# One-head attention: queries and keys through one folded matrix

## The chip, the cores and the metric

The kernel runs on one core of a Trainium2 chip. The metric is the time of one execution on the device in microseconds (us). The core has five engines with queues of their own that run in order and wait for each other by semaphores: TensorE (PE; PEld for its weight loads), VectorE (DVE), ScalarE (ACT), GpSimd (POOL) and SyncE (SP), which issues the DMAs.

## What is computed

Sixteen batches of 256 rows by 256 features pass through four conditioned blocks; the change touches the attention of the last one only. Cut to it, the reference is:

```
h = layernorm(x) * (1.0 + g1) + be1
Q = h @ Wq + bq
K = h @ Wk + bk
V = h @ Wv + bv
scores = einsum('bsd,btd->bst', Q, K) / sqrt(256)
attn = softmax(scores, axis=-1) @ V
x = x + a1 * attn
```

All weights are 256 by 256, there is one head, and everything is fp32.

## The kernel before

The work is done in eight stages, one behind the other, each over all 16 batches: feed-forward stages 0, 1, 3, 4, 5 and 7, a 16-head attention (2) and the one-head attention (6), which is meant here by "the stage". A batch is held as two tiles of 128 rows. To keep fp32 precision with the faster one-pass type (fp32r), every operand is split into a high part and the rest, its low part, and every product is three matmuls, low by high, high by low, high by high (`split3`, lines 290 to 292). So each matrix that TensorE makes is read twice from its bank: ScalarE writes the high part, VectorE the low part, and what needs the matrix waits for the low part.

The order of the work is written out by hand. The stage is a row of turns (`sh_turn`); in turn b, while batch b goes through its probabilities, batch b+1 goes through its projections and scores, and batch b+2 through its normalization. TensorE's order in a turn is: transposes of the normalized rows of b+2 (`ln_transpose`, line 418), query and key projection of b+1 (`sh_qk`), transposes of the probabilities of b (`sh_transpose`, line 1469), value projection of b+1 (`sh_v`), scores of b+1 (`sh_scores`), weighted sum of b (`sh_values`). VectorE's order is: statistics of b+3, reciprocal and scaling of b (lines 1501, 1503), residual update, low parts of queries and keys (line 1573), low part of the transposed probabilities (1483), low part of the values (1586), maximum of the scores (1489) and its scaled negative (1493), low part of the normalized rows (439), the next slice of the weights of stage 7 (328). GpSimd normalizes b+3 (367, 369, 377), makes the two residual additions (1217, 1209) and the low part of the weights (335). SyncE's queue loads the next slice of weights when GpSimd is done with the last one, and behind that the gate row of the batch (1222), for which GpSimd's line 1209 waits.

Ahead of the turns `sh_start` does the projections and the scores of batch 0. Ahead of that lies the last group of the feed-forward stage 5: at its end TensorE has two hidden chunks to multiply out (`ff_output`), and the head of the next stage is transposed in between; VectorE then updates the group's result (`ff_take`, line 648) and GpSimd adds it to x (665). `sh_v_hi` of batch 0 waits for those additions.

Of the kernel before, what the change touches and what calls it, by code (L numbers as in the profile page):

```python
# [23 lines left out]
P = 128  # L24
# [19 lines left out]
def bass_cond_blocks(nc, t, out):  # L44
# [62 lines left out]
    with ctx:  # L107
# [40 lines left out]
        gates = sb("gates", [P, 2 * GB, 2 * D], scope=ffn)  # L148
        ffn.close()
# [46 lines left out]
        be = sb("be", [P, 2, DC, BATCH])  # L196

# [42 lines left out]
        b_q = sem("b_q"); b_k = sem("b_k"); b_v = sem("b_v")  # L240
        q_hi = sem("q_hi"); q_lo = sem("q_lo"); k_hi = sem("k_hi"); k_lo = sem("k_lo")
# [23 lines left out]
        def after_attention(name, eng, p):  # L265

            values = HEADS * BATCH + (BATCH if p == L3_FF else 0)
            if name == "tensor":
                eng.wait_ge(w_lo, SLICE_BASE[p + 1])
                eng.wait_ge(exp_ready, values)  # L270
                if p == L3_FF:
                    eng.wait_ge(q_lo, BATCH)
                    eng.wait_ge(k_lo, BATCH)
# [473 lines left out]
        def ff_body(name):  # L747
            def body(eng, p, g, i, left):
# [20 lines left out]
                for c in range(C):  # L769
# [7 lines left out]
                    if name == "tensor":  # L777
# [10 lines left out]
                        ff_output(eng, p, g, i, c)  # L788
                    if name == "scalar":
# [7 lines left out]
                        if p == L3_FF and c == 1 and prev:  # L797
                            ff_gelu2(eng, p, g - 1)
                    if name == "vector":
# [28 lines left out]
                if name == "vector":  # L828
                    if ends:
                        head_unit(name, eng, p + 1, 0)  # L830
                    if last_norms:
# [3 lines left out]
                if name == "gpsimd":  # L835
                    if prev and p == L3_FF:
                        ff_gate2(eng, p, g - 1, 1 - i)
# [604 lines left out]
        qk1, kk1 = qk  # L1442
# [41 lines left out]

        def sh_max(dve, b):
# [24 lines left out]
        def sh_qk(pe, b, j, which):  # L1510
            (w, _) = w_tiles(S6)
            pe.wait_ge(ln_lo, S6 * BATCH + b + 1)
            B, lo, s = ((QB, q_lo, b_q), (KB, k_lo, b_k))[which]
            if not early(b, 1):
                pe.wait_ge(lo, b)
            for m in range(DC):
                for c in range(DC):
                    col = which * D + m * P
                    last = split3(pe, B[:, m * SEQ:(m + 1) * SEQ], [v[:, c, col:col + P] for v in w],
                                  [a[:, c, :] for a in a1[j]], c == 0, c == DC - 1)  # L1520
            last.then_inc(s, 1)
# [33 lines left out]
        QK_OF = ((QB, qk1, b_q, q_hi, q_lo, 0), (KB, kk1, b_k, k_hi, k_lo, DC))  # L1555

        def sh_qk_hi(act, b):
            for B, dst, mm, hi, _, at in QK_OF:
                act.wait_ge(mm, b + 1)
                act.wait_ge(s_mm, H0 + b)  # L1560
                for m in range(DC):
                    n = BIAS_AT[S6] + at + m
                    l = act.activation(dst[0][:, m * SEQ:(m + 1) * SEQ], B[:, m * SEQ:(m + 1) * SEQ],
                                       ACT.Identity, bias=vecs[:, n:n + 1])
                l.then_inc(hi, 1)

        def sh_qk_lo(dve, b):
            for B, dst, _, hi, lo, at in QK_OF:
                dve.wait_ge(hi, b + 1)
                for m in range(DC):  # L1570
                    n = BIAS_AT[S6] + at + m
                    cols = slice(m * SEQ, (m + 1) * SEQ)
                    l = dve.scalar_tensor_tensor(dst[1][:, cols], B[:, cols], vecs[:, n:n + 1],
                                                 dst[0][:, cols].bitcast(F32), ALU.add, ALU.subtract)
                l.then_inc(lo, 1)
# [33 lines left out]
        def sh_turn(name, eng, b, i, left):  # L1609
# [3 lines left out]
            if name == "tensor":  # L1613
                if b:
                    sh_ln(name, eng, b + 2, i)
                if left >= 1:
                    sh_qk(eng, b + 1, n, 0)
                    sh_qk(eng, b + 1, n, 1)
# [3 lines left out]
                if left >= 1:  # L1622
                    sh_v(eng, b + 1, n)
                    sh_scores(eng, b + 1)
                sh_values(eng, b, i)
            if name == "scalar":
                sh_scale1(eng, b)
                if left >= 1:
                    sh_qk_hi(eng, b + 1)
# [6 lines left out]
            if name == "vector":  # L1636
# [5 lines left out]
                if left >= 1:  # L1642
                    sh_qk_lo(eng, b + 1)
# [23 lines left out]
        def sh_start(name, eng):  # L1667
# [6 lines left out]
            for b in range(2):  # L1674
# [3 lines left out]
                if b == 0:  # L1678
                    if name == "tensor":
                        sh_qk(eng, 0, 0, 0)  # L1680
                        sh_qk(eng, 0, 0, 1)
                        sh_v(eng, 0, 0)
                    if name == "scalar":
                        sh_qk_hi(eng, 0)
                        sh_v_hi(eng, 0, 0)
                    if name == "vector":
                        sh_qk_lo(eng, 0)
                        sh_v_lo(eng, 0, 0)
            if name == "tensor":
                sh_scores(eng, 0)  # L1690
# [144 lines left out]
```

## Time and profile before

| | us |
|---|---|
| three runs, median | 1705.23 |
| lowest, highest | 1705.14, 1708.14 |
| the profiled execution | 1705.73 |
| its span, first to last instruction | 1703.9 |

| engine | busy, us | share of the span |
|---|---|---|
| TensorE, matmuls | 1618.7 | 95% |
| TensorE, weight loads | 1469.1 | 86% |
| VectorE | 1247.3 | 73% |
| ScalarE | 1181.5 | 69% |
| GpSimd | 941.0 | 55% |

The mean granted clock of TensorE is 0.982 of full speed. The shares are means over all stages; what the change is worth is read from the one stage and the end of the one ahead of it. Matmuls overlap, and their recorded ends are modelled, so that the distance from one start to the next says what a matmul costs, and its recorded length does not.

### The profile page before, as it was taken

The numbers are of one execution on the slowest core, as the hardware profiler recorded it, in microseconds if no ns is written. First come the engines' busy times: TensorE is split into PE (matmuls) and PEld (weight loads), VectorE is DVE, ScalarE is ACT, GpSimd is POOL, SyncE is SP. The second block draws the span as 40 slices with busy tenths as digits, with TensorE's granted clock in tenths as the row PEclk, the third lists the DMA queues.
The fourth block names the chain that finished last, engine by engine and source line by source line (L and its number), as shares of the span: only waits on it lengthen the run. The fifth ranks groups of instructions, "written<-read, shape, count | busy, mean of one in ns | idle before, by whom it ended". The sixth has DMA issues, their size and how long they took to land. (4 is left out here: it accounts for less than half of the span.)

```text
span 1703.9 us, 37905 instructions
## 1 busy us (share of the span) xinstructions
PE 1618.7 (95%) x13539; PEld 1469.1 (86%) x13539; DVE 1247.3 (73%) x2701; ACT 1181.5 (69%) x2944; POOL 941.0 (55%) x1139
## 2 busy tenths in 40 slices
PE   4888988999999999999999899999999999989997
PEld 2547878999999999999999789998888899979997
DVE  4766867888888888888888755556787778854442
ACT  3545657888888888888888665566667567756663
POOL 1555664666666666666666533323656578832222
PEclk7999999999999999999999899999999999999999
DMA  9223220000000000000000011111112212211111
GB/s 308 56 63 89 75 59 8 6 10 11 11 11 11 11 11 11 11 11 11 11 11 11 15 34 32 32 32 25 56 46 60 52 29 48 48 44 51 36 40 50
DMA packets 110974, 65.96 MB, mean 39 GB/s; under 512 B 81530, under 2 KB 92788, under 8 KB 110788
## 3 DMA queue, kind: packets, MB, share of 16 engines
q1 hardware_dynamic: 110788, 63.54, 13.9%
q8 instruction: 110, 1.80, 0.4%
q14 instruction: 76, 0.62, 0.1%
HBM read 59.06 MB, written 4.46 MB: 37 GB/s over the span
## 5 line engine op out<-in xcount | busy, mean ns | idle before, releaser
L1097 POOL TENSOR_TENSOR prob<-prob,rinv 128x512 f32<-128x512 f32 x254 | 259.1, 1041 | 51.1 <-DVE rinv L1078 51.1
L1069 ACT ACTIVATE prob<-s_banks,nmax 128x256 f32<-128x256 f32 x512 | 235.8, 475 | 6.7 <-DVE nmax L1059 6.7
L290 PE MATMUL bank<-WBhi,hl 128*128 128x256 f32 x768 | 219.2, 285 | 5.8 <-DVE upd L648 5.0
L291 PE MATMUL bank<-WBlo,hh 128*128 128x256 f32 x768 | 217.6, 283 | 0.0
L292 PE MATMUL bank<-WBhi,hh 128*128 128x256 f32 x768 | 215.4, 281 | 0.0
L611 ACT ACTIVATE hh<-bank,vecs 128x512 fp32r<-128x512 f32 x120 | 82.8, 690 | 154.0 <-PE bank L292 154.0
L1059 DVE TENSOR_REDUCE nmax<-s_banks 128x4 f32<-128x1024 f32 x128 | 156.4, 1222 | 45.0 <-issue 42.0
L1128 ACT ACTIVATE pthi<-bank 128x512 fp32r<-128x512 f32 x256 | 138.9, 595 | 69.0 <-PE bank L1118 68.6
L431 ACT ACTIVATE nThi<-bank,mod 128x256 fp32r<-128x256 f32 x192 | 110.4, 575 | 101.1 <-issue 75.6
L290 PE MATMUL bank<-aThi,WAlo 128*128 128x256 f32 x576 | 175.3, 304 | 2.4 <-DVE qklo L1026 2.4
L1133 DVE TENSOR_TENSOR ptlo<-bank,pthi 128x512 fp32r<-128x512 f32 x256 | 164.9, 686 | 4.4 <-ACT pthi L1128 0.5
L617 DVE TENSOR_TENSOR hl<-bank,hh 128x512 fp32r<-128x512 f32 x120 | 82.4, 688 | 112.2 <-ACT bank L611 111.2
L290 PEld LDWEIGHTS bank<-WBhi,hl 128*128 128x128 f32 x768 | 145.7, 190 | 18.5 <-issue 9.4
L291 PE MATMUL bank<-aTlo,WAhi 128*128 128x256 f32 x576 | 161.5, 280 | 0.0
L292 PE MATMUL bank<-aThi,WAhi 128*128 128x256 f32 x576 | 161.1, 280 | 0.0
L291 PEld LDWEIGHTS bank<-WBlo,hh 128*128 128x128 f32 x768 | 145.8, 190 | 6.9
L292 PEld LDWEIGHTS bank<-WBhi,hh 128*128 128x128 f32 x768 | 146.5, 191 | 0.0
L377 DVE TENSOR_SCALAR xn<-x,meanvar,rstd 128x256 f32<-128x256 f32 x224 | 120.9, 597 | 30.2 <-POOL rstd L369 30.2
L611 ACT ACTIVATE hh<-s_banks,vecs 128x512 fp32r<-128x512 f32 x120 | 84.2, 702 | 72.8 <-PE s_banks L292 72.1
L1144 PE MATMUL bank<-ptlo,vv 128*128 128x256 f32 x512 | 129.1, 285 | 4.6 <-DVE of L1170 4.6
L617 DVE TENSOR_TENSOR hl<-s_banks,hh 128x512 fp32r<-128x512 f32 x120 | 81.6, 680 | 70.6 <-ACT s_banks L611 70.6
L1177 POOL CAST oThi<-of 128x256 fp32r<-128x256 f32 x128 | 50.9, 397 | 141.2 <-DVE of L1170 140.3
(185 smaller groups left out, 5723.7 us busy)
## 6 DMA issues: line engine op xcount, KB each, us to landing
gates<-gate_scratch SPq DMA_DIRECT2D x96, 256.0 KB, 3.6
agate<-gate_scratch SPq DMA_DIRECT2D x32, 256.0 KB, 3.6
stage<-in_L_cond_W SPq DMA_DIRECT2D x64, 64.0 KB, 2.3
out<-x SPq DMA_DIRECT2D x16, 256.0 KB, 2.2
adaw<-in_L_cond_Wc SPq DMA_DIRECT2D x1, 3072.0 KB, 17.7
stage<-in_L_cond_W_qkv SPq DMA_DIRECT2D x8, 384.0 KB, 3.4
x<-in_x SPq DMA_DIRECT2D x1, 2560.0 KB, 16.6
stage<-in_L_cond_ff_w SPq DMA_DIRECT2D x32, 64.0 KB, 2.1
```

The lines of the kernel that those rows point to most:

```text
L290: pe.matmul(dst, lhs[1], rhs[0], start=start, stop=False, skip_group_check=True)
L291: pe.matmul(dst, lhs[0], rhs[1], start=False, stop=False, skip_group_check=True)
L292: return pe.matmul(dst, lhs[0], rhs[0], start=False, stop=stop, skip_group_check=True)
L377: last = eng.tensor_scalar(xn[j][:, k * D:(k + 1) * D], x[:, bass.ds(b * ROWW + k * D, D)], meanvar[:, j, k, 0:1], rstd[:, j, k:k + 1], AL ...
L611: last = act.activation(dst[:, :], U_BANKS[r][:, :], ACTF[p], bias=vecs[:, at:at + 1])
L617: dve.tensor_tensor(hl[r][:, :], U_BANKS[r][:, :], hh[r][:, :].bitcast(F32), ALU.subtract).then_inc(h_lo, 1)
L1059: dve.tensor_reduce(nmax[n % 2][:, :], s_banks[:, :, :].rearrange("p h (q k) -> p (h q) k", q=TPB), AX_X, ALU.max, negate=True).then_inc(n ...
L1069: last = act.activation(prob[h % 4][:, q, :], SB_[h % 2][:, q * SEQ:(q + 1) * SEQ], ACT.Exp, bias=of_head(nmax, h)[:, q:q + 1], accum_out= ...
L1097: pool.tensor_tensor(prob[h % 4][:, :, :], prob[h % 4][:, :, :], scale, ALU.mult).then_inc(prob_ready, 1)
L1128: act.activation(pt[h % 4][0][:, :], PTB[h % 2][:, :], ACT.Copy).then_inc(pt_hi, 1)
L1133: dve.tensor_tensor(pt[h % 4][1][:, :], PTB[h % 2][:, :], pt[h % 4][0][:, :].bitcast(F32), ALU.subtract).then_inc(pt_lo, 1)
L1144: last = pe.matmul(OB[:, h % 2 * SEQ:(h % 2 + 1) * SEQ], vv[:, c, h * P:(h + 1) * P], pt[h % 4][m][:, c * SEQ:(c + 1) * SEQ], start=c == 0 ...
```

## The change

The scores are written with one matrix: with h the modulated rows, Q K^T = (h (Wq Wk^T) + Wk bq) h^T + a term that depends on the query row alone, h Wq bk + bq bk. The changed kernel forms Wq Wk^T (`keyed`, split in high and low part, over a free piece of the weights' tile), Wk bq (`wkey`), Wq bk (`wrow`) and bq bk (`bdot`) once, at the end of stage 5: `fold_tensor`, `fold_scalar`, `fold_vector`. TensorE transposes the two weight matrices there in 16 steps, eight behind each of the output chunks 1 and 2, multiplies them in 12 matmuls behind chunk 3, and forms the vectors in 16 full-fp32 matmuls of one column and one of two.

In the stage, `sh_q` takes the place of the query projection, and the key projection, its two ScalarE and two VectorE operations and the wait of the scores for the keys are gone; the scores multiply by h itself. `sh_r` adds eight matmuls a batch, with parts of h as weights and two columns to stream, for the row term; `sh_row` takes it on VectorE in three operations. `sh_max` subtracts the row term from the scaled maximum and adds it again, in two operations where there was one.

```diff
         def sh_max(dve, b):
...
+            dve.wait_ge(r_scaled, b + 1)
+            dve.scalar_tensor_tensor(smax[0][:, :], smax[0][:, :], -SCALE1, rows_scaled[:, :], ALU.mult, ALU.subtract
+                                     ).then_inc(row_max, 1)
+            dve.wait_ge(row_max, b + 1)
             dve.wait_ge(exp_ready, n - 1)
-            dve.tensor_scalar(nmax[0][:, 0:TPB], smax[0][:, :], -SCALE1, None, ALU.mult).then_inc(nmax_ready, 1)
+            dve.tensor_tensor(nmax[0][:, 0:TPB], smax[0][:, :], rows_scaled[:, :], ALU.add).then_inc(nmax_ready, 1)
...
+        def sh_row(dve, b):
+
+            dve.wait_ge(b_r, b + 1)
+            dve.wait_ge(fold_cols, 3)
+            pairs = RB[:, 0:2 * TPB].rearrange("p (q v) -> p q v", v=2)
+            dve.tensor_copy(rowr[:, :], pairs[:, :, 0]).then_inc(r_taken, 1)
+            dve.wait_ge(r_taken, 2 * b + 1)
+            dve.scalar_tensor_tensor(rowr[:, :], pairs[:, :, 1], bdot[:, 0:1], rowr[:, :], ALU.add, ALU.add).then_inc(r_taken, 1)
+            dve.wait_ge(r_taken, 2 * b + 2)
+            dve.tensor_scalar(rows_scaled[:, :], rowr[:, :], SCALE1, None, ALU.mult).then_inc(r_scaled, 1)
...
+        def sh_r(pe, b, j):
+            if b:
+                pe.wait_ge(r_taken, 2 * b)
+            else:
+                pe.wait_ge(fold_cols, 3)
+            for q in range(TPB):
+                for c in range(DC):
+                    for a in a1[j]:
+                        last = pe.matmul(RB[:, 2 * q:2 * q + 2], a[:, c, q * P:(q + 1) * P], wrow[:, c, :],
+                                         start=c == 0 and a is a1[j][0], stop=c == DC - 1 and a is a1[j][1], skip_group_check=True)
+            last.then_inc(b_r, 1)
...
-        def sh_scores(pe, b):
+        def sh_scores(pe, b, j):
             pe.wait_ge(q_lo, b + 1)
-            pe.wait_ge(k_lo, b + 1)
...
                                   [m[:, c * SEQ + q * P:c * SEQ + (q + 1) * P] for m in qk1],
-                                  [m[:, c * SEQ:(c + 1) * SEQ] for m in kk1], c == 0, c == DC - 1)
+                                  [a[:, c, :] for a in a1[j]], c == 0, c == DC - 1)
...
+        def fold_vector(dve):
+
+            dve.tensor_tensor(bprod[:, :], vecs[:, BQ:BQ + DC], vecs[:, BK:BK + DC], ALU.mult).then_inc(fold_prod, 1)
+            dve.wait_ge(fold_hi, 1)
+            dve.tensor_tensor(keyed[1], FOLD_A[:, :].rearrange("p (k m) -> p k m", k=DC), keyed[0].bitcast(F32),
+                              ALU.subtract).then_inc(fold_lo, 1)
+            dve.wait_ge(fold_mm, 2)
...
+            for at, tiles, bias in ((0, wT[0:2], BK), (DC, wT[2:4], BQ)):
+                for m in range(DC):
+                    for d in range(DC):
+                        for v in tiles:
+                            pe.matmul(bank[6][:, at + m:at + m + 1], v[:, d * D + m * P:d * D + (m + 1) * P].bitcast(F32),
+                                      vecs[:, bias + d:bias + d + 1], start=d == 0 and v is tiles[0],
+                                      stop=d == DC - 1 and v is tiles[1], skip_group_check=True)
```

TensorE in a turn, before: the end of the key projection (`vv` holds the normalized rows of every second batch, `WAhi`, `WAlo` the weights), the transposes of the probabilities, the first matmul of the values.

```order
L290 MATMUL bank<-vv,WAlo 128x256
L291 MATMUL bank<-vv,WAhi 128x256
L292 MATMUL bank<-vv,WAhi 128x256
L1469 MATMUL bank<-ident,prob 128x128 x4
L290 MATMUL s_banks<-WAhi,vv 128x256
```

The same place now: the end of the one projection, the row term, the transposes, the values.

```order
L301 MATMUL bank<-vv,WAlo 128x256
L302 MATMUL bank<-vv,WAhi 128x256
L303 MATMUL bank<-vv,WAhi 128x256
L1629 MATMUL bank<-wrow,vv 128x2 x8
L1553 MATMUL bank<-ident,prob 128x128 x4
L301 MATMUL s_banks<-WAhi,vv 128x256
```

The twelve matmuls of the keys are gone, and eight of two columns stand between projection and transposes.

VectorE in the first turn, from the low parts of queries and keys (four operations) to the scaled maximum, before:

```order
L1573 SCALAR_TENSOR_TENSOR qklo<-bank,vecs,qkhi 128x256 x4
L1483 TENSOR_TENSOR ptlo<-bank,pthi 128x512
L1586 TENSOR_TENSOR vv<-s_banks,vv 128x512
L1489 TENSOR_REDUCE smax<-s_banks 128x2
L1493 TENSOR_SCALAR nmax<-smax 128x2
```

The same place now (`rowr`, `rows_scaled`: the row term):

```order
L1677 SCALAR_TENSOR_TENSOR qklo<-bank,wkey,qkhi 128x256 x2
L1574 COPY rowr<-bank 128x2
L1576 SCALAR_TENSOR_TENSOR rowr<-bank,bdot,rowr 128x2
L1578 TENSOR_SCALAR rows_scaled<-rowr 128x2
L1567 TENSOR_TENSOR ptlo<-bank,pthi 128x512
L1690 TENSOR_TENSOR vv<-s_banks,vv 128x512
L1584 TENSOR_REDUCE smax<-s_banks 128x2
L1588 SCALAR_TENSOR_TENSOR smax<-smax,rows_scaled 128x2
L1592 TENSOR_TENSOR nmax<-smax,rows_scaled 128x2
```

Two operations of 256 columns went, three of two columns came between the low parts, and one behind the maximum.

VectorE at the beginning of the stage, before: the last hidden chunk's low part, the low part of batch 0's normalized rows, then the update of the last feed-forward group (`upd`) and the statistics of batch 2.

```order
L617 TENSOR_TENSOR hl<-s_banks,hh 128x512
L439 TENSOR_TENSOR aTlo<-bank,aThi 128x512
L648 TENSOR_TENSOR upd<-bank,gates 128x512 x2
L354 BN_STATS stats<-x 128x6 x2
L360 BN_AGGR meanvar<-stats 128x2 x2
```

The same place now (`WAlo<-bank,WAhi` is the low part of the folded matrix):

```order
L628 TENSOR_TENSOR hl<-s_banks,hh 128x512
L450 TENSOR_TENSOR aTlo<-bank,aThi 128x512
L1515 TENSOR_TENSOR bprod<-vecs 128x2
L1517 TENSOR_TENSOR WAlo<-bank,WAhi 128x512
L1520 CAST wrow<-bank 128x2
L1521 COPY wkey<-bank 128x2
L1522 COPY bprod<-bank 128x2
L1524 TENSOR_TENSOR wrow<-bank,wrow 128x2
L1526 TENSOR_TENSOR bdot<-bprod 128x1
L659 TENSOR_TENSOR upd<-bank,gates 128x512 x2
L365 BN_STATS stats<-x 128x6 x2
```

Seven operations of the fold stand ahead of the update, and the second of them waits for ScalarE's high part of the product.

## Rows read from the trace of the kernel before

**Rows 1.** Stretches, one turn: us, busy time of each engine, clock, DMA share, GB/s
```profile
1431.47:1439.82 8.35, 8.32 (x70) 8.07 (x69) 6.82 (x19) 6.05 (x16) 6.97 (x8) 1.00 0.25 47
```

**Rows 2.** Timeline of TensorE, the same turn: start, us, line, operation
```profile
1431.47 0.60 PE L418 MATMUL bank<-ident,xn 128*128 128x128 f32 x4
...
1431.91 0.39 PE L290 MATMUL bank<-aThi,WAlo 128*128 128x256 f32 x1
...
1432.14 0.28 PE L291 MATMUL bank<-aTlo,WAhi 128*128 128x256 f32 x1
...
1434.83 0.60 PE L1469 MATMUL bank<-ident,prob 128*128 128x128 f32 x4
...
1435.19 0.36 PE L290 MATMUL s_banks<-WAhi,aTlo 128*128 128x256 f32 x1
...
1436.88 0.36 PE L290 MATMUL s_banks<-qkhi,qklo 128*128 128x256 f32 x1
...
1438.38 0.28 PE L290 MATMUL bank<-vv,ptlo 128*128 128x256 f32 x1
...
1439.82 0.60 PE L418 MATMUL bank<-ident,xn 128*128 128x128 f32 x4
```

**Rows 3.** Timeline of VectorE and ScalarE, the same turn, from the keys on
```profile
1435.90 0.88 DVE L1573 SCALAR_TENSOR_TENSOR qklo<-bank,vecs,qkhi 128x256 fp32r<-128x256 f32 x2 [0.53 <-ACT qkhi L1563]
...
1436.89 0.60 ACT L1582 ACTIVATE vv<-s_banks 128x512 fp32r<-128x512 f32 x1 [0.53 <-PE s_banks L292]
...
1437.52 0.69 DVE L1586 TENSOR_TENSOR vv<-s_banks,vv 128x512 fp32r<-128x512 f32 x1
```

**Rows 4.** One line's instructions: the score maxima; ns, first and last start
```profile
L1489 DVE TENSOR_REDUCE smax<-s_banks x16: 681/692/692, 1373.1 to 1497.1; 128x2 f32<-128x512 f32 x16
```

**Rows 5.** Timeline of the weight loads, where the scores begin
```profile
1428.49 0.19 PEld L290 LDWEIGHTS s_banks<-qkhi,qklo 128*128 128x128 f32 x1 [0.20 <-issue]
...
1428.60 0.19 PEld L291 LDWEIGHTS s_banks<-qklo,qkhi 128*128 128x128 f32 x1
```

**Rows 6.** Timeline of the weight loads, eight transposes with 16 columns
```profile
130.30 0.57 PEld L486 LDWEIGHTS bank<-ident,crow 16*128 16x128 f32 x8 [0.37 <-issue]
```

**Rows 7.** Timeline, small operations and the scaling of the probabilities
```profile
1432.99 0.13 DVE L1501 RECIPROCAL rinv<-rsum 128x2 f32<-128x2 f32 x1
...
1433.15 0.51 ACT L1508 ACTIVATE prob<-prob,rinv 128x256 f32<-128x256 f32 x1 [0.84 <-DVE rinv L1501]
...
1439.31 0.30 DVE L1493 TENSOR_SCALAR nmax<-smax 128x2 f32<-128x2 f32 x1
```

**Rows 8.** Timeline of GpSimd and of SyncE's queue, the same turn
```profile
1432.20 0.88 POOL L335 TENSOR_TENSOR WBlo<-stage,WBhi 128x128 fp32r<-128x128 f32 x2 [0.97 <-DVE WBhi L328]
...
1434.04 0.58 SPq L1222 DMA_DIRECT2D agate<-gate_scratch  x1
...
1438.29 1.30 POOL L1209 TENSOR_TENSOR axb<-x,agate 128x512 f32<-128x512 f32 x1
```

**Rows 9.** Timeline, from the last feed-forward group to the projection of batch 1
```profile
1360.55 0.66 PE L418 MATMUL bank<-ident,xn 128*128 128x128 f32 x4 [2.13 <-DVE xn L377]
...
1365.66 0.28 PE L290 MATMUL bank<-aThi,WAlo 128*128 128x256 f32 x1
...
1366.63 2.54 POOL L665 TENSOR_TENSOR x<-upd,xb 128x512 f32<-128x512 f32 x2 [3.58 <-DVE upd L648]
...
1370.08 0.60 ACT L1582 ACTIVATE vv<-s_banks 128x512 fp32r<-128x512 f32 x1 [0.58 <-PE s_banks L292]
...
1372.50 0.69 DVE L439 TENSOR_TENSOR vv<-bank,vv 128x512 fp32r<-128x512 f32 x1 [1.10 <-ACT bank L431]
...
1373.25 0.39 PE L290 MATMUL bank<-vv,WAlo 128*128 128x256 f32 x1 [1.08 <-DVE vv L439]
```

**Rows 10.** Timeline of TensorE, eight full-fp32 matmuls with 512 columns
```profile
109.33 3.61 PE L478 MATMUL bank<-adaw,condT 128*16 128x512 f32 x8
```

**Rows 11.** Stretches, columns as in rows 1, around the stage's beginning
```profile
1361.00:1363.00 2.00, 2.00 (x12) 2.00 (x11) 2.00 (x2) 1.71 (x4) 2.00 (x2) 0.53 0.00 0
```

More of the change, by code:

```diff
@@ L148, in bass_cond_blocks @@
         gates = sb("gates", [P, 2 * GB, 2 * D], scope=ffn)
+        fold = ExitStack()
+        wT = [sb(f"wT{i}", [P, DC * D], F32R, fold) for i in range(4)]
+        ones = sb("ones", [P, P], scope=fold)
+        fold.close()
         ffn.close()
@@ L788, in body @@
                         ff_output(eng, p, g, i, c)
+                        if ends and p == L3_ATTN - 1 and c:
+                            fold_tensor(eng, c)
                     if name == "scalar":
@@ L798, in body @@
                             ff_gelu2(eng, p, g - 1)
+                        if ends and p == L3_ATTN - 1 and c:
+                            fold_scalar(eng, c)
                     if name == "vector":
@@ L830, in body @@
                         head_unit(name, eng, p + 1, 0)
+                    if ends and p == L3_ATTN - 1:
+                        fold_vector(eng)
                     if last_norms:
@@ L835, in body @@
                 if name == "gpsimd":
+                    if first and p == L3_ATTN - 1:
+                        eng.memset(ones[:, :], 1.0).then_inc(fold_ones, 1)
                     if prev and p == L3_FF:
@@ new lines, in fold_scalar @@
+        def fold_scalar(act, c):
+            if c < 3:
+                for n in (2 * c - 2, 2 * c - 1):
+                    act.wait_ge(fold_tp, n + 1)
+                    act.activation(wT[n][:, :], FOLD_T[n % 2][:, :], ACT.Copy).then_inc(fold_read, 1)
+                return
+            act.wait_ge(fold_mm, 1)
+            act.activation(keyed[0], FOLD_A[:, :].rearrange("p (k m) -> p k m", k=DC), ACT.Copy).then_inc(fold_hi, 1)
+        def fold_vector(dve):
[4 more added lines that the diff above has]
+            dve.wait_ge(fold_mm, 2)
+            dve.tensor_copy(wrow[:, :, 0], bank[6][:, 0:DC]).then_inc(fold_whi, 1)
+            dve.tensor_copy(wkey[:, :], bank[6][:, DC:2 * DC])
+            dve.tensor_copy(bprod[:, :], bank[6][:, 2 * DC:3 * DC]).then_inc(fold_cols, 1)
+            dve.wait_ge(fold_whi, 1)
+            dve.tensor_tensor(wrow[:, :, 1], bank[6][:, 0:DC], wrow[:, :, 0].bitcast(F32), ALU.subtract).then_inc(fold_cols, 1)
+            dve.wait_ge(fold_cols, 1)
+            dve.tensor_tensor(bdot[:, :], bprod[:, 0:1], bprod[:, 1:2], ALU.add).then_inc(fold_cols, 1)
@@ L1553, in sh_values, with sh_q_hi, sh_q_lo @@
             last.then_inc(pv_mm, 1)
[L1555 to L1575, printed above, removed]
+        def sh_q_hi(act, b):
+            act.wait_ge(b_q, b + 1)
+            act.wait_ge(s_mm, H0 + b)
+            act.wait_ge(fold_cols, 3)
+            for m in range(DC):
+                l = act.activation(qk1[0][:, m * SEQ:(m + 1) * SEQ], QB[:, m * SEQ:(m + 1) * SEQ],
+                                   ACT.Identity, bias=wkey[:, m:m + 1])
+            l.then_inc(q_hi, 1)
+        def sh_q_lo(dve, b):
+            dve.wait_ge(q_hi, b + 1)
+            for m in range(DC):
+                cols = slice(m * SEQ, (m + 1) * SEQ)
+                l = dve.scalar_tensor_tensor(qk1[1][:, cols], QB[:, cols], wkey[:, m:m + 1],
+                                             qk1[0][:, cols].bitcast(F32), ALU.add, ALU.subtract)
+            l.then_inc(q_lo, 1)
         def sh_v_hi(act, b, j):
@@ L1642, in sh_turn @@
                 if left >= 1:
-                    sh_qk_lo(eng, b + 1)
+                    sh_q_lo(eng, b + 1)
+                    sh_row(eng, b + 1)
                 sh_pt_rest(eng, b)
```

80 lines of the change are left out of this document (59 added, 21 removed).

## The prediction

> **What bounds the kernel now.** I read the table of stretches first, for one turn of the one-head stage [rows 1]: in 8.35 us TensorE is busy for 8.32 us at full clock, its weight loads for 8.07, while VectorE has 6.82, GpSimd 6.97 and ScalarE 6.05. So the turn is TensorE's. The timeline of TensorE then gives the turn's parts [rows 2]: four transposes of the normalized rows 0.44 us, the two projections for queries and keys 2.92 (24 matmuls: 0.23 for the first, after the transposes, and from 1432.14 to 1434.83 0.117 for each other), four transposes of the probabilities 0.36, values projection 1.69, scores 1.50, weighted sum 1.44; together 8.35.
>
> Two of these hold a wait. The scores begin at 1436.88 although the values' 12 matmuls, 0.20 and eleven times 0.118, need only 1.50 of the 1.69: the low part of the keys ends on VectorE at 1435.90 + 0.88 = 1436.78 [rows 3], and that is what the scores wait for. That is the one stall that the change could remove beside the work itself. But right behind it stands another chain: values projection, ScalarE's copy at 1436.89 (0.60), VectorE's low part at 1437.52 (0.69), done at 1438.21 [rows 3]; the weighted sum, which needs it, starts at 1438.38. It has 0.17 to spare, no more.
>
> The stage has 16 turns; the score maxima run from 1373.1 to 1497.1 [rows 4], that is 124.0 us: 14 intervals of 8.35 and a first one of 7.1.
>
> **The change in a regular turn.** Removed: 12 matmuls of the key projection, 12 x 0.117 = 1.40 us of TensorE; two ScalarE activations and two VectorE operations of 0.88 in all, neither on the path; the wait for the low part of the keys.
>
> Added on TensorE: 8 matmuls with the activations as weights (128 columns) and two columns to stream. Their price is not in the trace, since every 128-column load of this type there hides behind 256 or more streamed columns. Three rows bound it. After a stall two such loads follow each other at 1428.49 and 1428.60 [rows 5]: 0.11 apart, with nothing streaming between them, so the load itself holds the pace. Eight transposes with 16 columns to stream took 0.57 us of loads, (0.57 - 0.136)/7 = 0.062 each [rows 6], but their loads are shorter (0.136 against 0.19 recorded). And 0.19 each is what it would be if every load ran to its recorded end before the next. I take 0.118: the spacing of 0.11, nearest because it is the same load, with some 0.01 for the change of weights. 8 x 0.118 = 0.94 a turn; bounds 0.50 and 1.52.
>
> The wait: with the keys gone, the scores start 0.28 sooner (0.20 of waiting and 0.08 of restart), and the weighted sum then waits for the low part of the values. That chain runs 3.06 us from the start of the values projection (1435.19 to 1438.25 [rows 2, 3]), plus 0.08 for the restart, against 3.19 now. So of 0.28 about 0.02 to 0.05 is left; I count 0.02.
>
> Added on VectorE: three operations on 128x2 for the row term, and one more behind the maximum. Such operations take 0.13 (the reciprocal) to 0.30 (the bias row) [rows 7]. Three cost 0.4 to 0.9, in place of the keys' 0.88 and of the 0.53 that VectorE waits for them [rows 3]; what hides them is the wait for the values' copy. If they took over 1.4, every turn would lose the excess. The one behind the maximum lengthens the way to the exponential by 0.2: now ScalarE scales the probabilities from 1433.15 to 1433.66 [rows 7] and TensorE transposes them at 1434.83 [rows 2], so there are 1.17 to spare; TensorE comes 0.46 sooner and this 0.2 later, which leaves 0.5.
>
> Turn: -1.40 + 0.94 - 0.02 = -0.48. Next in line is GpSimd, through the queue of SyncE: weights' low part ends at 1433.08, the gate row's DMA is issued at 1434.04 and landed when the addition starts at 1438.29 (1.30 long) [rows 8]; with the next low part (0.88) that is a circle of 5.21 + 1.30 + 0.88 = 7.39. No turn becomes shorter than about 7.4, so the gain ends at 0.95. At 7.87 it doesn't bind. 14 x -0.48 = **-6.7 us**.
>
> **The fold, ahead of the stage.** 16 transposes of the weights go into the two stretches in which TensorE waits anyway: 2.13 us of idle time before the transposes at 1360.55 [rows 9], and the wait for the last hidden chunk. Cost nothing; if the clock is low there, up to 1.0 us (below). ScalarE's four copies of 0.6 lie in its own idle time. Then, in place of the first projection at 1365.66 [rows 9]: 12 matmuls for the product, 1.40, to 1367.06; 16 matmuls with one column and one more, in full fp32, with 128-column weights. I price them like the loads above, 17 x 0.118 = 2.0 (bounds 17 x 0.062 = 1.1 and 17 x 0.43 = 7.3, the last from [rows 10], where such a matmul takes 3.61/8, about 0.43, with 512 columns), to 1369.07, 1369.24 with the signal. VectorE takes five small operations of about 0.2 for the columns and row vectors (1370.25), and only then, being in order, the update of the last feed-forward group that it did at 1365.86 before: one operation of 0.65 (1370.9), GpSimd's two additions of 2.54 in all (1373.45; they began at 1366.63 before [rows 9]). Behind these additions stands ScalarE's copy of the first values, which waits for them; it was at 1370.08. From there to the projection of batch 1 the way is unchanged: 1370.08 to 1373.25, 3.17 us over the modulation and VectorE's low part at 1372.50 [rows 9]. So that projection starts at 1373.50 + 3.17 = 1376.67: +3.4. The other way there, product, copy of 0.6, low part of 0.69, projection, row term and values, ends some 0.4 sooner. From the projection of batch 1 to its maximum 2.92 becomes 0.23 + 11 x 0.117 + 0.94 = 2.46: -0.46. At the end of the stage the extra operation behind the last maximum adds 0.2, since the last weights and the gate row hang on it.
>
> **Sum**: -6.7 + 3.4 - 0.5 + 0.2 = -3.6 against the profiled execution's 1705.73 (span 1703.9 and 1.8 around it): 1702.1. The median of the runs, 1705.23, lies 0.5 below that execution, so **1701.7**.
>
> The clock: from 1361 to 1363 it stood at 0.53 of full [rows 11], that is mostly at 1.2 GHz, after the idle time before 1360.55. With the transposes in that gap it may stay up, which gains nothing, since the last chunk comes at its own time; if it falls, the second eight transposes, up to 0.2 each then, push the last output matmuls by 1.0 or a little more. If the one-column matmuls let it fall, the first projection and the values, 2.9 us at full clock, lose 1 to 2. Both are in the range.
>
> **Rivals.** (A) *The small matmuls cost almost nothing.* At 0.062 or less each the turn is held by GpSimd's circle: 14 x -0.95 = -13.3, and with the start, the end and a first row term of 0.5 (+2.7) about 1694.6; halfway there about 1698. For it: [rows 6]. Against: [rows 5]. The Trainium skill, "TensorE: Matmul & The Clock Gate", section "Back-to-back issue gap", gives some 60 cycles (about 25 ns) for any matmul of 1 to 64 columns; by that rule this rival would come true. The rows disagree: even with 16 columns the spacing is 0.062.
>
> (B) *The fold is dear.* If every full-fp32 matmul costs 0.43 whatever its columns [rows 10], the chain ends 5.3 later: 1707.0; with two loads of 0.118 each 2.0 later, 1703.7; with the half clock 1703 to 1705. Against the 0.43: it was measured with 512 columns, and half of them streamed twice at the 0.117 of [rows 2] would give 4 x 0.117 = 0.47, so the streaming explains it and the loads need not. The Trainium skill, "FP8 and Floating Point Precision", section "TensorE Precision Notes", speaks of four passes through the array for true fp32; by that rule (B) would be likelier, while this trace shows the time of two passes.
>
> (C) *Slower: the loads of the eight small matmuls do not overlap.* If each takes its recorded 0.19, the row term costs 1.52 a turn, more than the 1.40 that the keys gave back: turns +0.10, 14 x 0.10 = +1.4, first turn +3.4 + 0.1, end +0.2: 1710.4. It turns to slower than before at 0.15 each. [Rows 5] speaks against it. Operations of 0.35 and more on VectorE would act in the same direction, at a smaller price.
>
> (D) *The turn stays as it is*, since the values' chain or the probabilities take the place of the projection: 1707 to 1709. By [rows 3, 7] neither can take more than 0.3 of a turn's 0.48.
>
> **How the numbers follow.** Forecast 0.62 (1699.5 to 1704, half of it on each side of 1701.8); (A) 0.13; (B) 0.14, half over 1705; (C) 0.09; (D) 0.02. A measurement of this kernel tells about 0.2%, 3.4 us, from no change, so faster means under 1701.8 and slower over 1708.6. Faster: 0.32 + 0.13 + 0.01 = 0.46. Slower: (C), 0.09. Same: the rest, 0.45. Range: without (C) and the far end of (A), 1697.0 to 1707.0.
>
> **What would show it.** In the profile of the changed kernel: the transposes of two following turns 7.9 apart (7.4: A; 8.4: C); loads of the row term 0.11 to 0.12 apart; no wait before the scores, a short one before the weighted sum; the projection of batch 1 some 3.4 us later than 1373.25, with the wait of ScalarE's first values copy put down to GpSimd. Wrong would be: a turn with TensorE idle on VectorE for more than 0.3, half clock inside the regular turns, or a fold whose one-column matmuls take over 4 us.

## The result and the profile after

The changed kernel takes 1715.86 us (median of 11 runs, 1709.67 to 1717.85) against 1705.46 for the kernel before (11 runs, 1701.59 to 1709.16): a ratio over all runs of 1.0051, interval 1.0041 to 1.0060 (the two medians alone give 1.0061). It is slower by half a per cent; the forecast was 1701.7, at most 1707. The profiled execution of after took 1710.98, one of the shortest of the 11, with a span of 1709.2; before it was 1705.73 with 1703.9.

The difference of the two spans, 5.3, splits by three marks, the update of the last feed-forward group but one, the first and the last score maximum of the stage:

| stretch | before | after | difference |
|---|---|---|---|
| to that update | 1353.11 | 1353.40 | +0.3 |
| update to first maximum: the fold and the first projections | 20.00 | 29.03 | +9.0 |
| first to last maximum: the turns | 123.97 | 119.12 | -4.9 |
| last maximum to the end of the span | 206.8 | 207.6 | +0.8 |

**The turns are of two lengths.** The maxima of after answer to [rows 4]; the table of stretches for a turn of each kind answers to [rows 1] (columns: us, busy time of TensorE, weight loads, VectorE, ScalarE, GpSimd, clock, DMA share, GB/s).

```profile
L1584 DVE TENSOR_REDUCE smax<-s_banks x16: 680/690/693, 1382.4 to 1501.5; 128x2 f32<-128x512 f32 x16
```

```profile
1422.19:1430.74 8.55, 7.71 (x66) 7.47 (x65) 7.40 (x20) 5.33 (x15) 6.99 (x9) 1.00 0.21 46
1463.18:1470.84 7.66, 7.66 (x66) 7.52 (x65) 7.01 (x20) 5.26 (x15) 6.95 (x9) 1.00 0.25 52
```

TensorE's work fell as meant, from 8.32 to about 7.7 a turn, at full clock. In the second row TensorE is busy throughout. In the first, TensorE stands still for 0.84 of 8.55, so the turn is longer than the old 8.35. From the maximum at 1396.54 to the one at 1447.82 there are six such turns, 8.55 each; behind it seven of 7.67.

The timeline of after around one long turn (start, us, engine, line, operation; in brackets the idle time ahead and its releaser), VectorE, then GpSimd, then TensorE:

```profile
1430.74 0.69 DVE L1584 TENSOR_REDUCE smax<-s_banks 128x2 f32<-128x512 f32 x1
1431.47 1.09 DVE L1588 SCALAR_TENSOR_TENSOR smax<-smax,rows_scaled 128x2 f32<-128x2 f32 x1
1432.59 0.16 DVE L1592 TENSOR_TENSOR nmax<-smax,rows_scaled 128x2 f32<-128x2 f32 x1
1432.67 0.68 DVE L450 TENSOR_TENSOR vv<-bank,vv 128x512 fp32r<-128x512 f32 x1
...
1431.26 1.28 POOL L1228 TENSOR_TENSOR axb<-x,agate 128x512 f32<-128x512 f32 x1
...
1433.40 0.38 PE L301 MATMUL bank<-vv,WAlo 128*128 128x256 f32 x1 [0.82 <-DVE vv L450]
```

The added operation behind the maximum (line 1588), two numbers a partition, takes 1.09, and it ends at 1432.56 where GpSimd's addition, begun 0.21 before it, ends (1431.26 + 1.28 = 1432.54). Behind it on VectorE stands the low part of the next batch's normalized rows (line 450), and TensorE's next projection waits 0.82 for that. GpSimd waits too: the casts of the next weights (line 339) stand on VectorE behind all this, and GpSimd's low part of these weights waits 1.16 for them:

```profile
1433.69 0.88 POOL L346 TENSOR_TENSOR WBlo<-stage,WBhi 128x128 fp32r<-128x128 f32 x2 [1.16 <-DVE WBhi L339]
```

Its busy time of 6.99, this wait and 0.40 of short gaps make up the 8.55. So the long turn is a circle of two engines: GpSimd's addition holds VectorE, and the casts that VectorE makes late hold GpSimd, whose next addition comes late by as much. Where the order is the other way round, the same operation takes 0.16:

```profile
1448.55 0.16 DVE L1588 SCALAR_TENSOR_TENSOR smax<-smax,rows_scaled 128x2 f32<-128x2 f32 x1
...
1448.82 1.29 POOL L1228 TENSOR_TENSOR axb<-x,agate 128x512 f32<-128x512 f32 x1 [0.62 <-DMA agate<-gate_scratch]
```

Here GpSimd's addition had waited 0.62 for the gate row and came 0.27 behind VectorE. From this turn on they are short.

**The fold** answers to [rows 9]. Timeline of after: TensorE, VectorE, GpSimd, ScalarE, TensorE.

```profile
1367.11 4.42 PE L1497 MATMUL bank<-vecs,wT 128*128 128x1 f32 x32
1371.39 0.56 PE L1500 MATMUL bank<-bprod,ones 128*128 128x2 f32 x2
1371.82 0.56 PE L301 MATMUL bank<-aThi,WAlo 128*128 128x256 f32 x1
...
1372.43 1.29 DVE L659 TENSOR_TENSOR upd<-bank,gates 128x512 f32<-128x512 f32 x2
...
1373.20 2.51 POOL L676 TENSOR_TENSOR x<-upd,xb 128x512 f32<-128x512 f32 x2 [9.84 <-DVE upd L659]
...
1379.03 0.60 ACT L1686 ACTIVATE vv<-s_banks 128x512 fp32r<-128x512 f32 x1 [3.38 <-PE s_banks L303]
...
1382.57 0.39 PE L301 MATMUL bank<-vv,WAlo 128*128 128x256 f32 x1 [1.18 <-DVE vv L450]
```

```profile
1360.00:1369.00 9.00, 7.79 (x66) 7.55 (x66) 5.46 (x7) 3.76 (x8) 3.21 (x3) 1.00 0.01 2
1369.00:1371.00 2.00, 2.00 (x15) 2.00 (x14) 0.00 (x0) 0.00 (x0) 0.00 (x0) 0.69 0.00 0
1371.00:1380.00 9.00, 9.00 (x43) 9.00 (x44) 4.30 (x17) 1.56 (x4) 5.92 (x6) 0.50 0.00 0
1380.00:1382.00 2.00, 1.39 (x12) 1.18 (x10) 0.53 (x2) 1.98 (x5) 0.00 (x0) 1.00 0.01 4
```

The second fence is the table of stretches, columns as above. The 16 one-column matmuls stand as 32 records and take 4.4; during them the granted clock falls from 1.00 to 0.50 (from 2.4 to 1.2 GHz), though TensorE is recorded as busy all the time, and it stays there through the whole first projection, its row term and the values, until 1380. The projection of batch 1 starts at 1382.57, 9.3 later than before.

### The profile page after: what moved, and what is told of

It is laid out like the page before. It is cut to its first block and busy times, and to the rows that moved or that the text cites. A ratio compares the mean times of both kernels' runs of the same rounds, so it can differ in the third digit from the quotient of the medians.

```text
span 1709.2 us, 37919 instructions
## 1 busy us (share of the span) xinstructions
PE 1620.6 (95%) x13537; PEld 1472.6 (86%) x13537; DVE 1253.3 (73%) x2740; ACT 1173.9 (69%) x2917; POOL 941.9 (55%) x1140
## 3 DMA queue, kind: packets, MB, share of 16 engines
q1 hardware_dynamic: 110788, 63.54, 13.7%
## 5 line engine op out<-in xcount | busy, mean ns | idle before, releaser
L301 PE MATMUL bank<-aThi,WAlo 128*128 128x256 f32 x544 | 166.9, 307 | 4.9 <-DVE aTlo L450 2.5
L302 PE MATMUL bank<-aTlo,WAhi 128*128 128x256 f32 x544 | 153.0, 281 | 0.0
L303 PE MATMUL bank<-aThi,WAhi 128*128 128x256 f32 x544 | 152.6, 281 | 0.0
```

The costliest lines, as they stand in the source:

```text
L301: pe.matmul(dst, lhs[1], rhs[0], start=start, stop=False, skip_group_check=True)
L302: pe.matmul(dst, lhs[0], rhs[1], start=False, stop=False, skip_group_check=True)
L303: return pe.matmul(dst, lhs[0], rhs[0], start=False, stop=stop, skip_group_check=True)
```

## Experiments

All times below are medians. Each ratio is taken over all runs, against runs of the kernel before on the same chip (medians from 1704.22 to 1706.38), and can differ by up to 0.1% from the quotient of the medians. The edits are shortened to what matters. Two questions: what makes a turn long, and what makes the fold dear.

**The maximum's path as before.** The operation with the row term behind the maximum goes; line 1592 becomes the scaling of before. The row term is formed and not used (it is the same for all keys of a query, so the softmax removes it).

```
-dve.scalar_tensor_tensor(smax, smax, -SCALE1, rows_scaled, ALU.mult, ALU.subtract)
-dve.tensor_tensor(nmax, smax, rows_scaled, ALU.add)
+dve.tensor_scalar(nmax, smax, -SCALE1, None, ALU.mult)
```

> The changed kernel, with the scaled negative of the maximum made in one operation as before; the row term is still formed and taken from its bank, but not used (it cancels in the softmax). Theory A (the operation of VectorE that takes both operands from SBUF stands still until GpSimd's addition of 1.29 us is over): no operation between maximum and exponential is over 0.35 us, all regular turns take 7.6 to 7.8 us instead of 8.55 in the long ones, and the time falls to 1702 to 1707. Rival B (the long operation is only a sign that VectorE waits; GpSimd's circle with the gate row's DMA holds the turn): the turns stay at 8.4 to 8.6 and the time at 1714 to 1717.

Measured: 1712.94, ratio 1.0042 (1.0026 to 1.0057), single executions from 1703.6 to 1714.3. The profiled one was the shortest; its line of the scaling, and the same operation with GpSimd's addition in one turn:

```profile
L1588 DVE TENSOR_SCALAR nmax<-smax x16: 168/168/175, 1382.1 to 1495.6; 128x2 f32<-128x2 f32 x16
```

```profile
1426.60 0.17 DVE L1588 TENSOR_SCALAR nmax<-smax 128x2 f32<-128x2 f32 x1
...
1426.88 1.28 POOL L1228 TENSOR_TENSOR axb<-x,agate 128x512 f32<-128x512 f32 x1
```

All turns were short there, with VectorE 0.28 ahead of GpSimd in the one shown. That the median stayed at 1713 spoke against the added operation as the only culprit; a second profile of the same kernel was to show a long execution.

> The changed kernel with the maximum's path of before, all in SBUF, once more, for a look at an execution of 1711 to 1714: the first look fell on its fastest one (1703.6), in which the scaling behind the maximum took 0.17 in all 16 batches. Theory (the scaling, from SBUF to SBUF, is held by GpSimd's addition in some executions and not in others): where the profiled execution is at 1711 to 1714, the scaling takes 0.9 to 1.1 in the turns that are 8.5 long and ends with the addition, and 0.17 in the short ones. Rival (another operation or a load is late): turns of 8.3 to 8.5 with the scaling at 0.17 to 0.35. An execution of 1702 to 1705 with 0.17 throughout would tell nothing new.

Measured: 1711.45, ratio 1.0041 (1.0027 to 1.0055), and this time a profile of an execution with long turns:

```profile
L1588 DVE TENSOR_SCALAR nmax<-smax x16: 170/1084/1116, 1378.2 to 1500.5; 128x2 f32<-128x2 f32 x16
```

```profile
1425.57 1.08 DVE L1588 TENSOR_SCALAR nmax<-smax 128x2 f32<-128x2 f32 x1
...
1425.35 1.28 POOL L1228 TENSOR_TENSOR axb<-x,agate 128x512 f32<-128x512 f32 x1
```

The same operation, now 0.22 behind GpSimd's start, is held to GpSimd's end (1426.65 and 1426.63). Its maxima are 8.3 apart. So it is not the added operation as such: the old scaling, also with all operands in SBUF, is held too, and who starts first decides.

**One operand in PSUM.** The scaled row term is kept in two free columns of a PSUM bank. Nothing is left out; TensorE's next row term waits until VectorE has read these columns.

```
-rows_scaled = sb("rows_scaled", [P, TPB])
+rows_scaled = bank[1][:, 8:8 + TPB]
 def sh_r(pe, b, j):
+    pe.wait_ge(nmax_ready, H0 + b)
```

> The changed kernel, with the scaled row term kept in free columns of a PSUM bank instead of SBUF, so that both operations behind the maximum have one operand in PSUM; TensorE's next row term waits until they are done. Same operations, same order, same waits on VectorE. Theory A: the first of the two takes under 0.4 us in every turn, turns 7.6 to 7.8, time 1702 to 1707. Rival B, or a wait that comes from the place in the order and not from the operands: 1.1 us as before in the long turns, time 1712 to 1717.

Measured: 1704.09, ratio 0.999 (0.998 to 1.0); 11.8 below the changed kernel. The added operation and the maxima, by line:

```profile
L1588 DVE SCALAR_TENSOR_TENSOR smax<-smax,bank x16: 156/156/157, 1382.0 to 1495.5; 128x2 f32<-128x2 f32 x16
L1584 DVE TENSOR_REDUCE smax<-s_banks x16: 682/691/692, 1381.2 to 1494.8; 128x2 f32<-128x512 f32 x16
```

Never held, all regular turns 7.6 to 7.7.

**The old scaling with its source in PSUM**: the maximum's path of before once more, with the maximum written to PSUM.

```
-dve.tensor_reduce(smax, S1, AX_X, ALU.max)
-dve.tensor_scalar(nmax, smax, -SCALE1, None, ALU.mult)
+dve.tensor_reduce(bank[1][:, 8:10], S1, AX_X, ALU.max)
+dve.tensor_scalar(nmax, bank[1][:, 8:10], -SCALE1, None, ALU.mult)
```

> The changed kernel with the maximum's path of before (maximum, one scaling by -1/16, exponential; the row term is formed and then unused), as in the run in which that path stood in SBUF and gave times from 1703.6 to 1714.3; here the maximum is written to PSUM, so that the scaling reads PSUM and not SBUF. Theory (the short turns are lost whenever a small VectorE operation behind the maximum with SBUF operands alone meets GpSimd's addition and is held by it; the scaling of 0.17 too): the scaling is never held, all turns stand 7.60 to 7.70 apart, every run lies at 1702 to 1705, and the scatter of the SBUF version is gone. Rival (the slow runs of the SBUF version come from something else, such as the order in which the turns happened to fall in): median 1711 to 1714 as there, single runs from 1703 to 1714.

Measured: 1703.14 (1697.81 to 1704.8, 11 runs), ratio 0.9986 (0.9977 to 0.9995). The scatter towards 1714 is gone, and the scaling is never held:

```profile
L1589 DVE TENSOR_SCALAR nmax<-bank x16: 158/159/160, 1381.0 to 1494.4; 128x2 f32<-128x2 f32 x16
```

**A quarter of the one-column sums** in the fold, so the clock and the fold's length are tried apart from the turns. The kernel leaves out three quarters of the sums for the bias vectors.

```
-for d in range(DC):
-    for v in tiles:
-        pe.matmul(bank[6][:, at + m], v[d, m], vecs[:, bias + d], ...)
+pe.matmul(bank[6][:, at + m], tiles[0][0, m], vecs[:, bias], ...)
```

> The changed kernel with 4 of the 16 one-column matmuls of the fold; three quarters of the sums for the bias vectors are left out. Theory A' (these matmuls cost by their loads, two each at 0.134, and leave TensorE's clock to fall for the first projection and values): the first maximum starts at 1375 to 1377 instead of 1382.4, and the clock stays at 2.4 GHz through the first projection; the time is 5 to 7 below the changed kernel at the same number of long turns. Rival (the loads alone, no clock): the first maximum at 1379 to 1380.

Measured: 1710.23, ratio 1.0025 (1.0015 to 1.0035). Table of stretches, maxima by line, and the groups of VectorE from 1380 to 1502 (busy us, mean ns):

```profile
1369.00:1371.00 2.00, 2.00 (x20) 2.00 (x19) 1.79 (x7) 0.84 (x2) 2.00 (x2) 1.00 0.00 0
1371.00:1380.00 9.00, 7.66 (x66) 7.38 (x65) 5.94 (x21) 6.61 (x15) 6.55 (x9) 1.00 0.00 1
```

```profile
L1581 DVE TENSOR_REDUCE smax<-s_banks x16: 682/691/692, 1374.9 to 1500.2; 128x2 f32<-128x512 f32 x16
```

```profile
L1585 DVE SCALAR_TENSOR_TENSOR smax<-smax,rows_scaled 128x2 f32<-128x2 f32 x15 | 15.8, 1051 | 0.5
```

The clock stays at 1.00 and the first maximum comes 7.6 earlier than in after; counted from the update at 1352.45 it is 22.4 in place of 29.0, so 6.6 are the fold's. Yet nearly all turns were long here (mean 1.05 for the held operation), from the first maximum to the last 125.4 against 119.1 in the profiled execution of after, and 6.2 went there.

**The fold alone**, put into the kernel before, its results unused; queries and keys are projected as before.

```
 (kernel before)
+fold_tensor / fold_scalar / fold_vector in the last feed-forward group
+sh_qk, sh_v of batch 0: wait for the fold
```

> The kernel before, with the whole fold at the end of stage 5 added and its results not used: query and key projections as before. It prices the fold alone. Theory A': regular turns 8.35 as before, the first maximum 9 to 11 later than 1373.1, time 1714 to 1717. If the fold cost only what the prediction gave it (3.4 and the key projection beside it): 1709.

Measured: 1714.43, ratio 1.0051 (1.0039 to 1.0063): +8.0. The fall of the clock is there, somewhat shorter (0.69 from 1371 to 1380, in after 0.50); the first maximum comes 8.4 later than before, a little less than the theory's 9 to 11; and the turns are those of before (1381.5 to 1505.4, 123.9):

```profile
1369.00:1371.00 2.00, 2.00 (x15) 2.00 (x14) 0.00 (x0) 0.00 (x0) 0.00 (x0) 0.68 0.00 0
1371.00:1380.00 9.00, 8.97 (x54) 8.76 (x54) 5.08 (x16) 3.25 (x8) 5.91 (x6) 0.69 0.00 1
```

```profile
L1573 DVE TENSOR_REDUCE smax<-s_banks x16: 683/692/692, 1381.5 to 1505.4; 128x2 f32<-128x512 f32 x16
```

**Both causes taken away**: the PSUM operand and the quarter of the sums, the two edits above together.

> Both causes taken away at once: the row term's pair of operations reads PSUM, and 4 of the 16 one-column sums of the fold are left (three quarters of the bias sums are left out). Theory (two separate costs that add): 1704.1 - 7.6 = 1696.5, within 1695 to 1698; first maximum at 1374 to 1376, turns 7.60 to 7.70. Rival (the earlier start meets the same end, as the turns are then bound by loads or by GpSimd, or the turns fall back to 8.5): 1701 to 1705.

Measured: 1697.27, ratio 0.9949 (0.9937 to 0.9962). That is within 1 of the sum: the two costs are separate and add; without them the kernel stands some 8 below the one before.

```profile
L1581 DVE TENSOR_REDUCE smax<-s_banks x16: 680/691/692, 1374.3 to 1487.7; 128x2 f32<-128x512 f32 x16
```

**Without the row term.** The bias column alone is made, by 8 short fp32r matmuls behind the fold's first transposes; the maximum goes through PSUM. VectorE's update of the last feed-forward group now stands ahead of the low part of the folded matrix, and no longer behind the whole fold.

```
-sh_r, sh_row; the 17 small fp32 matmuls; wrow, bprod, bdot, rowr, rows_scaled
+bqs = high and low part of the query bias, two columns
+for m, d, v in wT[2:4]: pe.matmul(bank[2][:, 2*m:2*m+2], v[d, m], bqs[:, d, :], ...)
+dve.tensor_reduce(wkey, bank[2] pairs, AX_X, ALU.add)
```

> The row term left out altogether (it is the same number for all keys of a query, so the softmax removes it and the result is the same): no row-term matmuls, no three VectorE operations on them, and the maximum's path of before with the maximum in PSUM; the bias column of the projection is made by 8 short matmuls in the fold's second chunk, beside its transposes, in place of 33 behind it. Theory (fold's columns and clock cost 7.6; the row term's 0.81 on TensorE and its VectorE operations are the rest of the turn): first maximum at 1373.5 to 1375, turns 7.4 to 7.5, the time 1692 to 1695. Rival (turns of 7.65 are GpSimd's and the loads' already, so the row term itself costs nothing): turns stay at 7.60 to 7.70, 1695.5 to 1697.5. Against both: if the clock falls in the fold without the one-column sums too, the first maximum comes after 1379 and the time is 1699 or more.

Measured: 1696.32, ratio 0.9948 (0.9935 to 0.996): the rival. The clock stayed at 1.00 through the fold, the first maximum came at 1374.2, but the turns stayed at 7.66 although TensorE now stood still for 0.74 of the turn from 1436.00 to 1443.66. VectorE, then GpSimd, in one of them:

```profile
1442.87 0.92 DVE L334 CAST WBhi<-stage 128x128 fp32r<-128x128 f32 x2
...
1442.29 1.28 POOL L1225 TENSOR_TENSOR axb<-x,agate 128x512 f32<-128x512 f32 x1
1443.88 0.88 POOL L341 TENSOR_TENSOR WBlo<-stage,WBhi 128x128 fp32r<-128x128 f32 x2 [0.30 <-DVE WBhi L334]
```

The turn is GpSimd's: busy 6.96, and 0.30 of its idle time is a wait for two casts on VectorE, which its own addition holds (0.92 for the two; 0.35 where they run undisturbed).

**The gate row first.** As the last kernel, with the two loads of a turn in the other order.

```
-weights_load(eng, S6 + 1, b)
 gate_load(eng, S6, b, BATCH + b)
+weights_load(eng, S6 + 1, b)
```

> The kernel without the row term, and SyncE loads the gate row of the next batch ahead of the weights slice, not behind it. Theory (in short turns GpSimd's addition waits 0.4 to 0.6 for the gate row, so the load's place is the next bound): that wait is gone, turns 7.1 to 7.3, the time 2 to 4 under the kernel without the row term. Rival (the turn is bound by TensorE's and VectorE's chain or by GpSimd's busy time of 7.1 to 7.4, not by that wait): within 1 of it; or longer by up to 3, where the weights slice that now comes later is waited for.

Measured: 1693.61, ratio 0.9933 (0.9919 to 0.9947), 2.7 below the last. The time lies in the theory's range, but by luck, for the theory falls: the turns are 7.66 to 7.68 as there (maxima from 1371.2 to 1484.3, 113.1, against 1374.2 to 1487.3), and of the 4.4 between the two profiled spans 3.0 stand ahead of the stage, where both run the same instructions. What the 2.7 are is open.

**The casts on ScalarE**, again against the kernel without the row term.

```
 (scalar) sh_exp(eng, b + 1)
+(scalar) wait for the slice; activation(WBhi, stage, Copy)
-(vector) weights_hi(eng, S6 + 1, b)
```

> The kernel without the row term; the next sublayer's weights slice is rounded to its upper part by ScalarE behind the exponential, not by VectorE, where the two casts are held by GpSimd's addition (0.92 for what takes 0.35 alone) and GpSimd then waits 0.30 for them. Theory (the turn of 7.66 is GpSimd's circle, busy 7.0 and that wait among its gaps): turns 7.35 to 7.45, the time 1691.5 to 1693.5. Rival (the turn is the chain through TensorE, VectorE and ScalarE, with GpSimd following): turns 7.6 to 7.7, 1695.5 to 1697.5, or up to 2 more if the two casts delay ScalarE's scaling of the probabilities.

Measured: 1690.51 (1688.88 to 1694.41), ratio 0.9927 (0.9915 to 0.9939): 13.7 below the kernel before, the shortest of all, and better than both kernels of this comparison. GpSimd's wait is gone. The maxima span 105.6 in place of 113.0; the regular turns take 6.9 to 7.5, in the mean 7.10 in place of 7.66:

```profile
1445.53 1.29 POOL L1232 TENSOR_TENSOR axb<-x,agate 128x512 f32<-128x512 f32 x1
1446.78 0.89 POOL L348 TENSOR_TENSOR WBlo<-stage,WBhi 128x128 fp32r<-128x128 f32 x2
```

```profile
L1582 DVE TENSOR_REDUCE bank<-s_banks x16: 689/700/700, 1372.8 to 1478.4; 128x2 f32<-128x512 f32 x16
```

Both turns and time fell below the theory's 7.35 to 7.45 and 1691.5 to 1693.5. Of the 0.6 that a turn lost, 0.34 lies between the starts of GpSimd's addition and of its low part of the weights (1.59 with the casts on VectorE, 1.25 here), and 0.25 between that low part and the second operation behind it (1.42 and 1.17); why these also follow more closely was not tried.

## Why the prediction was wrong

**The keys' matmuls and the row term: right.** The row term's 8 matmuls in a regular turn go from 1434.90 to the transposes at 1435.71, 0.81 in place of the 0.94 taken (they start 0.11 apart); rivals A and C, which priced them at 0.5 and 1.52, are out. Where nothing is held, the turn fell from 8.35 to 7.66, and the sum had 7.87.

```profile
1434.90 0.95 PE L1629 MATMUL bank<-wrow,vv 128*128 128x2 f32 x8
1435.71 0.55 PE L1553 MATMUL bank<-ident,prob 128*128 128x128 f32 x3
```

**The operation behind the maximum: the step that failed.** The prediction said "The one behind the maximum lengthens the way to the exponential by 0.2", with 0.5 to spare. Both halves were wrong. Its price is not 0.16 to 0.3 but up to 1.09, since it is held until GpSimd's addition ends. And the way with the least to spare was another. In the kernel before, VectorE's next operation is the low part of the normalized rows, and TensorE's next projection needs it:

```profile
1439.52 0.68 DVE L439 TENSOR_TENSOR vv<-bank,vv 128x512 fp32r<-128x512 f32 x1
...
1440.26 0.38 PE L290 MATMUL bank<-vv,WAlo 128*128 128x256 f32 x1
```

It ended at 1440.20, 0.06 ahead of the projection, which itself followed four transposes without a stop. The prediction named who waits for the exponential and not what is queued behind on VectorE. The hold could be read ahead of time too: the scaling in [rows 7] ends at 1439.61 and the addition in [rows 8] at 1439.59, and over the stage that scaling took more than its shortest time:

```profile
L1493 DVE TENSOR_SCALAR nmax<-smax x16: 169/304/349, 1373.8 to 1497.8; 128x2 f32<-128x2 f32 x16
```

So in the kernel before VectorE meets the last 0.13 of the addition in a typical turn; with the projection of the keys gone it meets nearly all of it, or none. The 0.30 of [rows 7] was used as the price of a small operation, and it was 0.17 of work and 0.13 of waiting. Long turns cost 125.4 between the first and the last maximum (the kernel with a quarter of the sums), short ones 113.6 (the row term in PSUM): 11.8, as much as lies between the medians of after and of the PSUM version. The sum had 116.8 for this stretch (124.0 - 6.7 - 0.5). The profiled execution of after had seven short turns; by these figures an execution with none would be 6.2 longer, an estimate of 1717.2 beside the highest measured time of 1717.85.

The Trainium skill, "SBUF — State Buffer", section "Who interferes with whom", states the rule: a VectorE operation with two inputs in SBUF, or one such as a scaling or cast in its two-port mode, shares ports with a GpSimd operation that reads SBUF, and the one that comes second is blocked until the first is done. The trace agrees: 1.09 and 1.08 with all operands in SBUF, 0.16 in every batch with one in PSUM. (In which mode the scaling ran, no trace shows.)

**The fold: the mechanism was right, two sizes were not.** The transposes lay in TensorE's idle time as said, and with them the clock stayed at 1.00 where [rows 11] had 0.53. The small matmuls were priced at 17 x 0.118 = 2.0 and took 4.7 to the first projection (1367.11 to 1371.82). The price of a load was right, the number of loads was not: each full-fp32 matmul stands as two records with a load each, 0.112 apart at full clock, so 34 loads come to 3.8 (a case of rival B); the last ones run at half clock, 0.213 apart. The trace of before could have told it. [Rows 10] are four matmuls and not eight: line 478 issues four for each 512 columns, one for each 128 of the weight's 512 rows, three times in all, which is 12 matmuls for the 24 records of this line:

```profile
L478 PE MATMUL bank<-adaw,condT x24: 592/592/604, 109.3 to 126.3; 128*16 128x512 f32 x24
```

So one of them takes 3.61/4 = 0.90, and not 0.43; one pass over 512 columns takes 0.23 beside it (fp32r, two starts in a row), so the trace shows the time of about four passes, where the prediction read two:

```profile
108.31 0.40 PE L292 MATMUL bank<-nThi,WAhi 128*128 128x512 f32 x1
108.54 0.40 PE L290 MATMUL bank<-nThi,WAlo 128*128 128x512 f32 x1
```

The first projection started 2.6 later than the step had it. "If the one-column matmuls let it fall" the clock was to cost 1 to 2; it fell, and from the first projection to that of batch 1 it took 10.75 in place of the step's 7.43, so 3.3. Together 5.9, which is the 9.3 measured less the 3.4 predicted; 0.3 of it stands ahead of the fold. The copy of the first values was to wait for GpSimd; it waited 3.38 for TensorE, since at half clock the way over projection, row term and values became the longer one. With a quarter of the sums the clock stayed up and the stretch from the update to the first maximum was 22.4, 2.4 over before; the step, with 12 of its 17 small matmuls taken out, gives 3.4 - 12 x 0.118 = 2.0.

**The sum.** In an execution with long turns the turns lie 8.6 over the prediction's sum (125.4 against 116.8) and the fold 5.9: 14.5 together, against the 14.2 between the median and the forecast. Two of the three signs that the prediction named for being wrong came: TensorE idle on VectorE for more than 0.3 (0.82), and one-column matmuls of over 4 us (4.42); half clock inside the regular turns did not.

Rival B (fold dear, up to 1707) named the fold's part, with a chance of 0.14 and nearly the size. "Slower" had 0.09, all of it for (C), which was not the cause. No rival named the hold; (D) asked whether the turn might stay as it was and looked at two chains, neither of them this one. The floor of GpSimd's circle, given as 7.39, is 7.66 as long as the casts are on VectorE, by the same hold: at 7.66 the row term's 0.81 on TensorE cost nothing. At 7.66 the circle does not run through SyncE's queue, as the prediction had it: with the gate row first the turns stayed. With the casts on ScalarE they went to 7.10, under the floor.

What stays open is what sets an execution on the long or the short turns, and why the small matmuls let the clock fall. The rows show that each kind keeps itself going, with 0.2 to 0.3 between GpSimd's and VectorE's starts either way, and in after a late gate row ended the long ones; what began them was not tried.

## What to carry to other kernels

Before an operation is added on VectorE, look at what GpSimd does at that time and where the operands lie: a small operation between SBUF tiles can cost as much as GpSimd's whole addition, and one operand in PSUM avoids it. A step's slack is the least over all that stands behind it on its engine, not that of its own result alone. Small matmuls at the edge of a stage are priced with the clock that they leave behind: here the work after them lost more than they took over their estimate.

## What the runs showed of the hardware

- VectorE's operations on 128x2 with all operands in SBUF, whether with two tensor inputs (1.09) or one (1.08), were held to the end of a GpSimd addition that had begun 0.2 earlier; with one operand in PSUM the same took 0.16 in all 16 batches. Two casts of 128x128 took 0.92 in place of 0.35 in the same situation.
- The hold made turns of two lengths, 7.66 and 8.55, in one execution. Executions of one kernel with the scaling in SBUF lay from 1703.6 to 1714.3; with its source in PSUM none of 11 lay over 1704.8 (the lowest at 1697.81).
- TensorE was granted half its clock in the course of 16 full-fp32 matmuls with one column, while it was recorded as busy all the time, and for some 8 us of other matmuls behind them (1371.8 to 1380); with 4 of the 16, or with 8 short fp32r matmuls between transposes in their place, the clock stayed at 1.00. Whether the one column or the full fp32 does it was not tried.
- A full-fp32 matmul stands in the trace as two records, each with a weight load: 32 for the 16 with one column, 0.11 apart at full clock and 0.21 at half; 24 for 12 with 512 columns, 0.90 a matmul against 0.23 in one pass.
